# Pre-norm transformer layer on one core: the order of loads, sums and statistics at the joints of the feed-forward part, and the last division of attention on VectorE

## What is computed

```python
x = x + attn(layernorm(x), qkvw, qkvb, ow, ob)     # softmax(q k^T / sqrt(32)) v, then ow
y = layernorm(x)
x = x + (silu(y @ W_gate.T) * (y @ W_up.T)) @ W_down.T
```

## Time and profile before

| | |
|---|---|
| median of 3 runs | 3092.87 us (3090.59 to 3095.39) |
| the profiled execution | 3092.47 us |
| its span | 3090.7 us |
| TensorE busy | 3002.1 us, 97% |
| VectorE busy | 2276.9 us, 74% |
| ScalarE busy | 1652.7 us, 53% |
| POOL busy | 1188.7 us, 38% |
| chain that ended last, TensorE's share | 81% |

### The profile page before, as it was taken

The page is one execution under the profiler, slowest core; times in us unless marked ns, Lnnn a source line. Parts: engine busy times, 40 slices in busy tenths (PEclk is TensorE's granted clock), DMA queues, the critical chain, the costliest instruction groups (busy, mean ns, idle before and its releaser), DMA issues.

```text
span 3090.7 us, 38986 instructions
## 1 busy us (share of the span) xinstructions
PE 3002.1 (97%) x13728; PEld 2351.0 (76%) x13728; DVE 2276.9 (74%) x3403; ACT 1652.7 (53%) x3031; POOL 1188.7 (38%) x860
## 2 busy tenths in 40 slices
PE   7999999999999999999899999999999999999999
PEld 7766777766777677676667778888878888788787
DVE  6798888998899898898987477765565556455653
ACT  2478787877788787887766143332322223332231
POOL 1234334433344343343333234444344444444730
PEclk9999999999999999999999999999999999999999
DMA  3434333343343433433643845632442223667874
GB/s 117 126 110 135 88 116 113 101 144 107 104 135 85 127 100 104 139 92 97 212 123 119 259 137 179 197 122 102 184 164 102 102 103 114 227 194 230 264 247 133
DMA packets 287139, 437.05 MB, mean 141 GB/s; under 512 B 30752, under 2 KB 166048, under 8 KB 276576
## 3 DMA queue, kind: packets, MB, share of 16 engines
q1 hardware_dynamic: 286944, 434.56, 44.2%
HBM read 297.61 MB, written 136.31 MB: 140 GB/s over the span
## 4 chain that ended last, share of the span: by engine, by line
PE 81%; DVE 11%; ACT 2%; DMA 2%; POOL 2%; issue 1%; SPq 1%; ACTq 0%
PE ps L839 19%; PE ps L840 19%; PE ps L841 19%; PE ps L911 6%; PE ps L930 6%; PE ps L942 6%; PE ps L947 6%; DVE mx L1283 4%; DVE pl L1305 3%; POOL traw L1544 1%; DVE wl L1255 1%; SPq L1559 1%; ACT ph L1065 1%; ACT pu L1064 1%; PE ps L872 1%
## 5 line engine op out<-in xcount | busy, mean ns | idle before, releaser
L1064 ACT ACTIVATE pu<-ps 128x512 f32<-128x512 f32 x1024 | 617.5, 603 | 339.3 <-PE ps L930 336.2
L1480 POOL TENSOR_TENSOR pl<-pu,ph 128x512 fp32r<-128x512 f32 x315 | 429.3, 1363 | 952.0 <-ACT ph L1065 951.4
L1283 DVE TENSOR_REDUCE mx<-ps 128x1 f32<-128x512 f32 x1024 | 696.5, 685 | 118.1 <-PE ps L911 107.6
L1065 ACT ACTIVATE ph<-ps 128x512 fp32r<-128x512 f32 x1024 | 616.2, 602 | 0.0
L1305 DVE TENSOR_TENSOR pl<-pu,ph 128x512 fp32r<-128x512 f32 x709 | 554.0, 782 | 57.7 <-ACT ph L1065 54.6
L839 PE MATMUL ps<-bh,gh 128*128 128x512 f32 x1208 | 472.3, 391 | 7.4 <-DVE gu L1402 2.5
L841 PE MATMUL ps<-bl,gh 128*128 128x512 f32 x1208 | 471.6, 390 | 0.0
L840 PE MATMUL ps<-bh,gl 128*128 128x512 f32 x1208 | 471.4, 390 | 0.0
L911 PE MATMUL ps<-kst,qst 96*128 96x512 f32 x1024 | 415.9, 406 | 21.2 <-DVE mx L1283 20.0
L930 PE MATMUL ps<-qst,kst 98*128 98x512 f32 x1024 | 410.1, 401 | 6.0 <-ACT ph L1065 5.2
L942 PE MATMUL ps<-ph,vt 128*65 128x512 f32 x1024 | 412.3, 403 | 0.8 <-ACT uu L1071 0.8
(11 more groups left out here) (139 smaller groups left out, 5236.2 us busy)
## 6 DMA issues: line engine op xcount, KB each, us to landing
graw<-in_wgu SPq DMA_DIRECT2D x42, 1024.0 KB, 5.2
sraw<-a_d SPq DMA_DIRECT2D x56, 704.0 KB, 5.0
wraw<-in_wqkv SPq DMA_DIRECT2D x24, 1024.0 KB, 5.5
qst<-q_d SPq DMA_DIRECT2D x192, 128.0 KB, 2.9
kst<-k_d SPq DMA_DIRECT2D x192, 128.0 KB, 3.0
a_d<-hs SPq DMA_DIRECT2D x88, 256.0 KB, 2.1
traw<-in_wd SPq DMA_DIRECT2D x77, 256.0 KB, 5.3
tt<-in_wd SPq DMA_DIRECT2D x77, 256.0 KB, 5.3
```

The source lines that it names most:

```text
L1064: e.activation(pu[sl][:, :], bk[:, :], ACT.Exp, scale=SCALE).then_inc(s["a_p"], 1)
L1065: e.activation(ph[sl][:, :], bk[:, :], ACT.Exp, scale=SCALE).then_inc(s["a_ph"], 1)
L1283: e.reduce_max(mx[:, j % 2, t, half:half + 1], ps[2 + bank_of["a", j, t, half]][:, :], AX.X).then_inc(s["v_mx"], 1)
L1480: e.tensor_tensor(pl[sl][:, :], pu[sl][:, :], ph[sl][:, :], ALU.subtract).then_inc(s["g_pl"], 1)
```

## The change

Five edits, four of them to the list of steps:

1. `cdiv` of the last chunk goes from POOL to VectorE, with a semaphore `v_cs`. The units between `cin`, `cdiv`, `ch`, `cl` and `cst` of that chunk are 8, 2, 2, 1 in place of 7, 4, 1, 1, and `marks` ends with 2376 in place of 2400, which leaves one group of the projection more for the time after attention.
2. `ostat` of the last token tile (15) comes after product 6 of unit 0 in place of right behind its `osum`.
3. `gs` is asked for two products sooner and makes three sums; the fourth is a step of its own, `gs4`, behind `gsp` of operand 1.
4. At the joint of up/gate and down the loads and sums of slices 11 and 12 stand ahead of the last `ast`, and `hin(3)` stands at the head of visit 0.
5. `TAKEN` becomes 0, 2, 4, 5, 7, 8, 10, 11, 11, and the eleventh slice of a pass is split in visit 0 of its own pass. Of the waits for `a_d` stores in front of a slice's load, those stay that guard shared tiles.

```diff
-TAKEN = [0, 2, 4, 6, 8, 10, 11, 11, 11]
+TAKEN = [0, 2, 4, 5, 7, 8, 10, 11, 11]
...
-    follow["cin"] = lambda c, half: [(14 if c < B * KT - 1 else 7, ("cdiv", c, half))]
-    follow["cdiv"] = lambda c, half: [(5 if c < B * KT - 1 else 4, ("ch", c, half))]
-    follow["ch"] = lambda c, half: [(2 if c < B * KT - 1 else 1, ("cl", c, half))]
+    follow["cin"] = lambda c, half: [(14 if c < B * KT - 1 else 8, ("cdiv", c, half))]
+    follow["cdiv"] = lambda c, half: [(5 if c < B * KT - 1 else 2, ("ch", c, half))]
+    follow["ch"] = lambda c, half: [(2 if c < B * KT - 1 else 2, ("cl", c, half))]
...
-    follow["osum"] = lambda n, half: [(1, ("ostat", n)), (1, ("ystore", n))] if half else []
+    follow["osum"] = lambda n, half: [(1, ("ostat", n))] * (n < B * TT - 1) + [(1, ("ystore", n))] if half else []
...
                     defer(5, "gs", 0)
+                    defer(12, "gs4", 0)
...
-    marks = [(0, 112), (190, 960), (238, 1184), (262, 1280), (462, 2144), (512, 2400)]
+    marks = [(0, 112), (190, 960), (238, 1184), (262, 1280), (462, 2144), (512, 2376)]
...
+    then(0, 6, ("ostat", B * TT - 1))
...
     for i, (u, q) in enumerate(order):
+        v, r = order[min(i + AHEAD_G + 2, len(order) - 1)]
+        if r == 0 and v % NF < NU:
+            step("gs", v)
...
-                    if r == 0 and v:
-                        step("gs", v)
                     split.add((v, r))
                     step("gsp", v, r)
+                    if v and r == 1 and v % NF < NU:
+                        step("gs4", v)
...
     step("hs", hidden // 2 - 1)
+    for f in range(2):
+        step("tload", CH + f)
+        step("tadd", CH + f)
     step("ast", hidden // 2 - 1)
...
+        if v == 0:
+            step("hin", 3)
         if q < 6:
             for f in range(TAKEN[j], TAKEN[j + 1]):
-                step("tload", CH * (q + 1) + f)
-                if len(PARTS[q + 1]) > 1:
-                    step("tadd", CH * (q + 1) + f)
+                if q or f > 1:
+                    step("tload", CH * (q + 1) + f)
+                    if len(PARTS[q + 1]) > 1:
+                        step("tadd", CH * (q + 1) + f)
             for f in range(TAKEN[j - 2], TAKEN[j - 1]) if j > 1 else ():
                 step("tsp", CH * (q + 1) + f)
+        if q and j == 0:
+            step("tsp", CH * (q + 1) - 1)
...
-        if v + 3 < visits:
+        if 3 < v + 3 < visits:
             step("hin", v + 3)
...
+                elif what == "cdiv":
+                    c, half = at_
+                    if c == B * KT - 1:
+                        dve.wait_ge(f"d_c{half}", 96 if half else 96 * of_part(c, half))
+                        e.tensor_tensor(ca[half][:, :], ca[half][:, :], cb[half][:, :], ALU.add).then_inc(s["v_cs"], 1)
+                        dve.wait_ge("v_cs", 2 * half + 1)
+                        e.tensor_tensor(ca[half][:, :], ca[half][:, :], cr[half][:, :], ALU.mult).then_inc(s["v_cs"], 1)
...
                         sp.wait_ge("g_t", of_combined(m - 3))
-                        for i in (3, 2, 1, 6, 4, 5, 0):
-                            sp.wait_ge(f"d_a{i}", 16 * CH * B)
+                        if (m - CH) % 3 == 2:
+                            for i in (3, 2, 1, 6):
+                                sp.wait_ge(f"d_a{i}", 16 * CH * B)
```

More of the change, by code:

```diff
@@ L657 @@
         "p_a", "v_mx", "v_mm", "p_m", "v_mh", "v_ml", "d_m0", "d_m1", "p_st", "a_p", "a_ph", "g_pl", "v_pl", "p_pv",
-        "a_u", "d_u0", "d_u1", "d_z0", "d_z1", "v_r", "d_r0", "d_r1", "d_c0", "d_c1", "g_cs", "a_ch", "v_cl", "d_cs",
+        "a_u", "d_u0", "d_u1", "d_z0", "d_z1", "v_r", "d_r0", "d_r1", "d_c0", "d_c1", "g_cs", "v_cs", "a_ch", "v_cl", "d_cs",
         "d_o0", "d_o1", "a_oh", "v_ol", "d_bo", "d_ct0", "d_ct1", "d_ct2", "d_xr0", "d_xr1", "d_xr2", "g_xr", "p_o", "v_o", "v_os",
@@ L1076, in act_program @@
                     i = int(n == 2 * B * KT)
-                    act.wait_ge("g_cs", 2 * n)
+                    if c == B * KT - 1:
+                        act.wait_ge("v_cs", 2 * (half + 1))
+                    else:
+                        act.wait_ge("g_cs", 2 * n)
                     bias = bqkv_c[:, 2 * KT + c % KT:2 * KT + c % KT + 1]
@@ L1484, in pool_program @@
                     n = of_part(c, half)
-                    i = int(n == 2 * B * KT)
-                    pool.wait_ge(f"d_c{i}", 96 if i else 96 * n)
-                    e.tensor_tensor(ca[i][:, :], ca[i][:, :], cb[i][:, :], ALU.add).then_inc(s["g_cs"], 1)
-                    pool.wait_ge("g_cs", 2 * n - 1)
-                    e.tensor_tensor(ca[i][:, :], ca[i][:, :], cr[i][:, :], ALU.mult).then_inc(s["g_cs"], 1)
+                    if n < 2 * B * KT - 1:
+                        pool.wait_ge("d_c0", 96 * n)
+                        e.tensor_tensor(ca[0][:, :], ca[0][:, :], cb[0][:, :], ALU.add).then_inc(s["g_cs"], 1)
+                        pool.wait_ge("g_cs", 2 * n - 1)
+                        e.tensor_tensor(ca[0][:, :], ca[0][:, :], cr[0][:, :], ALU.mult).then_inc(s["g_cs"], 1)
                 elif what == "xbo":
@@ L1499, in pool_program @@
                     if u % NF < NU:
-                        (a11, a12), (a21, a22) = ([graw[u % 2][:, kind, 4 * k:4 * k + 4, :] for k in range(2)] for kind in range(2))
+                        a11, a21, a22 = (graw[u % 2][:, kind, 4 * k:4 * k + 4, :] for kind, k in ((0, 0), (1, 0), (1, 1)))
                         s0, s1 = (gs[u % 2][n][:, :, :] for n in range(2))
@@ L1512, in pool_program @@
                         e.tensor_tensor(s1, s0, a11, ALU.subtract).then_inc(s["g_s"], 1)
-                        pool.wait_ge("g_s", of_weights(u, 2))
-                        pool.wait_ge("v_gl", of_operand(u, 1))
-                        e.tensor_tensor(s1, a12, s1, ALU.subtract).then_inc(s["g_s"], 1)
+                elif what == "gs4":
+                    u, = at_
+                    s1 = gs[u % 2][1][:, :, :]
+                    pool.wait_ge("g_s", of_weights(u, 2))
+                    pool.wait_ge("v_gl", of_operand(u, 1))
+                    e.tensor_tensor(s1, graw[u % 2][:, 0, 4:8, :], s1, ALU.subtract).then_inc(s["g_s"], 1)
                 elif what == "hs":
@@ L1800, in sp_program @@
                     sp.wait_ge("g_y", n - 3 if n >= 4 else 0)
+                    for a in (4, 5):
+                        sp.wait_ge(f"d_a{a}", 16 * CH * B)
                     copy(yb[n % 4][:, :], y_d[b, tile_of(i + t), halves(nh)], f"d_yi{n % 4}")
```

## The result

The changed kernel takes 3099.52 us (median of 14 runs, 3095.94 to 3104.99); the kernel before took 3092.05 us in the runs beside it. The ratio is 1.0027 (95% interval 1.0019 to 1.0034): 0.2 to 0.3% slower, at the edge of what a measurement of this kernel can tell. The prediction was 3093.3 us, range 3080 to 3101.5. So the time lies in the range, 6.2 us above the forecast, and it is the slower side that it had at 0.27.

What follows compares the result with a forecast made beforehand. TensorE is busy nearly all the time, so only its waits or lowered clock move the end. Gains of -16.6 us and costs of +17.4 gave +0.8 on the profiled 3092.47 us: 3093.3 us, range 3080 to 3101.5.

Steps and rivals of the forecast that it cites:

- The last slice: Down part: split behind the hidden tile, each pass's last slice stalls TensorE for `tl`, six times; +13.3 us, plus +4.1 low clock.
- The clock: Down part: 2.4 of the six new stalls drop TensorE's clock, 1.7 us each; +4.1 us, bounds 0 and 10.2.
- Rival (b): Down part: the clock falls behind all six last-slice stalls, 10.2 us in place of 4.1, giving 3099.4 us; chance 0.13.
- The hand-over: Start of the down part: loading visit 3's hidden tile ahead of six Wd loads removes its stall and low clock; -8.4 us.
- Visit 31: Down part: the new TAKEN lets this visit's load leave sooner, ending a 2.6 us stall with its overlap; -2.8 us.
- The second batch's start: Gate/up: weight sums asked for sooner stand ahead of `hs` on POOL, ending a 2.5 us `gu` stall; -3.0 us.
- "No wait for `gu`": Sign for the second batch's start in gate/up: TensorE's list of waits should hold no wait for a gate/up sum.
- The division: Attention's end: last division to VectorE and eight projection steps moved behind attention; -2.4 us, bounds -5 and +2.5.
- the moved steps: Attention's end: eight projection steps leave it, 4.6 us gained, and are done afterwards, 5.45 us; +0.85 together.
- the present stall's end: Attention's end: the 3.57 us stall for `xr`, its low clock and a 0.6 us wait for `ct` go; -6.2 us.
- VectorE's new stall: Attention's end: VectorE's division ahead of `osum(5,1)` makes TensorE 2.2 us late, plus 0.7 for a possible low clock; +2.9.

Runs made afterwards that it cites:

- e1: The whole change, but with the last slice's split ahead of the hidden tile's in visit 0 of a pass: 3079.33 us, ratio 0.9961 to the kernel before.
- e7: The kernel of e1 with VectorE's part of the second batch's third block one product later: 3072.14 us, ratio 0.9947 to the kernel before.
- e4: The kernel before with only the weights' sums changed, three asked for two products sooner and the fourth a separate step: 3089.92 us, ratio 0.9993.
- e5: The kernel before with the last chunk's division on VectorE, its new units and 2376 in marks, statistics unmoved: ratio 0.9990.
- e6: The kernel before with only 2376 for 2400 in marks, the division staying on POOL: ratio 0.9986.
- e2: The kernel before with only the new TAKEN table and the last slice split in its own pass, behind the hidden tile: 3111.95 us, ratio 1.0062.
- e3: The kernel before with only the joint to the down part changed (slices 11 and 12 and hidden tile 3 sooner), old TAKEN: 3083.96 us, ratio 0.9977.

## Why the prediction was right, and where it was not

**The last slice (forecast +13.3 and +4.1 us; measured 23.0 together).** The mechanism was right, the place in the queue, the six stalls and their group in the list; its size was not. The idle time with the overlaps is 15.1 + 6 x 0.17 = 16.1 us, 2.8 above the term. In passes 1 and 2 `tl` was taken at 0.69 us from the earlier trace rows. That row was read at a place where POOL was idle. Now it runs beside POOL's sums of the new slices and takes 1.75 (in passes 3 to 6 it is 0.68):

```profile
2717.71 1.63 DVE L1448 TENSOR_TENSOR sl<-sraw,sh 128x1408 fp32r<-128x1408 f32 x1 [4.82 <-ACT sh L1170]
2719.25 1.75 DVE L1454 TENSOR_TENSOR tl<-traw,th 128x512 fp32r<-128x512 f32 x1
...
2718.34 3.80 POOL L1572 TENSOR_TENSOR traw<-traw,tt 128x512 f32<-128x512 f32 x2 [10.16 <-DMA tt<-in_wd]
```

Twice 1.06 is 2.1 of the 2.8 us. Most of the rest is the load of pass 6, which took 3035.16 - 3028.14 = 7.0 us to `sh` in place of 6.4:

```profile
3028.14 0.52 SPq L1587 DMA_DIRECT2D sraw<-a_d  x1
...
3035.16 1.38 ACT L1170 ACTIVATE sh<-sraw 128x1408 fp32r<-128x1408 f32 x1 [7.29 <-DMA sraw<-a_d]
```

**The clock (inside the term above: +4.1 taken, 6.9 measured).** This step was wrong in its count, not in its price. A fall behind a stall of such length cost 1.7 us again. But 2.4 of six were taken from five stalls of 1.85 to 2.6 us, while the real stalls were 2.9, 2.9, 1.8, 1.7, 1.9 and 3.9 us. The four that fell are the three longest and the 1.9. Rival (b), all six, would have given 3099.4; the measured 3099.5 is reached by four falls and longer stalls, so that agreement is chance.

**The hand-over (-8.4).** Right. In the changed kernel `sraw` for visit 3 is issued at 2663.26, 11.9 us after the down part's first matmul, as worked out (2669.1 - 2657.23). Alone the edit gave 8.0 us. Its load took 4.9 us to `sh` and not the 8.3 that was allowed for. The six loads of W_down are no longer right ahead of it, which is the likely reason; no run tested that alone:

```profile
2663.26 0.52 SPq L1587 DMA_DIRECT2D sraw<-a_d  x1
...
2668.20 1.38 ACT L1170 ACTIVATE sh<-sraw 128x1408 fp32r<-128x1408 f32 x1 [8.55 <-DMA sraw<-a_d]
```

**Visit 31 (-2.8).** Right: no wait there in the changed kernel or in e1, and 2.2 to 2.6 us in the six kernels with the old table. The stalls of visit 31 and of the hand-over, with the low clock behind the latter, make up the 10.9 us by which the down part of the kernel before exceeds 419.0.

**The second batch's start (-3.0).** About right in sum, wrong in mechanism. "No wait for `gu`" was the sign to look for, and there is one of 2.2 us. The prediction did see that the sums now run beside VectorE's split and took 1.2 us for it, within bounds of 0 and 3. What it missed is who waits: VectorE's `gu` stands behind that split, and TensorE needs it at once; in e7, with the split one product later, the wait is gone. Over gate/up, the three profiled executions with the new order that have no other edit there took 837.73 to 838.94 us, the six with the old one 840.02 to 841.85, so 2.6 us is what the traces show, and e4's median shows 2.1 without being clear of no change.

**The division (-2.4).** Right in sum (-3.0 in e5), wrong in where the gain comes from. The sum had the moved steps at +0.85, the present stall's end at -6.2 and VectorE's new stall at +2.9 (1.9 us idle measured, no low clock). The new stall belongs to VectorE's division, but the old stall's end belongs to the moved steps: e6 has all of it and no new stall. They work through SP's queue, where their loads no longer stand ahead of `r_d`; the prediction had that term, but booked it to the new stall alone. With the kernel taken apart this way the last edit is two, one worth about 5 us and one that costs 1 to 2. Here `ca` was asked for 2.7 us after `r_d` was issued (1691.92 - 1689.25), close to the 2.8 taken from the rows. The Trainium skill's fixed cost of about 2.0 us (page "DMA: Bandwidth & Descriptors", section "Anatomy of one DMA") would have made the stall 1.4 us, by the prediction's estimate. That section is on DMAs that GpSimd issues and these are SP's, so the comparison says nothing against it.

**The sum.** The medians of the parts alone add up: +20.0 (e2), -8.0 (e3), -2.1 (e4), -3.0 (e5) give +6.9; the change as a whole is +7.5. Of the 6.2 us that the time lies above the forecast, 5.6 are the last slice's (23.0 against 17.4). The statistics that moved to product 6 of unit 0 are only in the change itself and in e1 and what is built on it; nothing in those traces shows a cost of them, and they were not timed apart.

## What to carry to other kernels

When a step moves, look at what it now queues behind: the whole loss of 20 us here came from one split placed behind a neighbour whose data were still on their way, and swapping the two lines made the same change 0.4% faster than before. Take the duration of an operation from a row with the same neighbours on the other engines, since beside them it can take more than twice as long (0.68 and 1.75 us here). A step that moves takes its loads along: eight projection steps, put behind attention, cleared SP's queue for the store that everything waited for. And take apart an edit that does two things, because here one half of the edit to the division earned what the other half partly gave back.

## What the runs showed of the hardware

VectorE's operations on two SBUF tiles take 0.68 us for 128x512 alone and 1.3 to 1.8 us beside one of POOL's: `gl` 0.69 and 1.32, `gz` 0.69 and 1.78, `tl` 0.68 and 1.75; in pass 4, beside POOL's longest row of sums, 3.47 us for two. POOL's own, 1.29 us alone, take 1.6 to 2.7 us beside VectorE's. VectorE's sum with an operand in PSUM (`block_z`) keeps its 0.68 us in the midst of POOL's row. From e7_block_later:

```profile
2887.39 3.47 DVE L1454 TENSOR_TENSOR tl<-traw,th 128x512 fp32r<-128x512 f32 x2
2890.79 0.68 DVE L1472 TENSOR_TENSOR block_z<-ps,block_y 128x512 f32<-128x512 f32 x1
...
2861.47 30.55 POOL L1572 TENSOR_TENSOR traw<-traw,tt 128x512 f32<-128x512 f32 x17
```

The Trainium skill, page "SBUF — State Buffer", section "SBUF: two separate sides", says that VectorE and GpSimd share a pair of ports that one instruction locks for its whole length, and that a VectorE operation with two SBUF inputs and a GpSimd operation that reads SBUF have to wait for each other there. The trace agrees: 1.75 us is 0.68 and most of a POOL operation of 1.29.

The clock: the 14 traces have 74 stalls of TensorE of more than 1 us behind attention. Of the 17 with 1.0 to 1.7 us idle none was followed by the low clock, of the 10 up to 2.0 three (1.85, 1.86 and 1.95 us), of the 22 up to 2.4 ten, of the 6 up to 2.7 four, and of the 19 that were longer (2.76 to 6.24 us) all. The same stall at the first batch's start, 2.32 or 2.33 us long in every execution that has it, was followed by it in five of ten. A fall cost 1.6 to 1.7 us behind stalls up to 4.1 us, and 1.7 to 2.9 behind longer ones (what the matmuls behind it took above their usual 0.227 us, summed). So the price of a stall here is its length with the 0.17 us of overlap, sometimes 1.7 us more from 1.85 us on, and 1.7 or more in each of the 19 cases of 2.76 us and above.
